# Order of the steps around the convolution, the last tiles of the dense stage and experts 0 and 1, in an adaptive-norm, gated-recurrence and mixture-of-experts block

## Chip, cores and metric

One core of one Trainium2 chip. The time is device time in microseconds (us) from start to end of one execution. Before the change it is 294.07 us, the median of three runs (293.27 to 294.33).

## What is computed

Four sequences of 256 tokens with 256 features (1024 tokens). A conditioning vector gives six modulation rows per sequence. Then

```python
h = layernorm(x) * (1 + ca) + sa
x = x + ga * attn(h)
h = layernorm(x) * (1 + cb) + sb
x = x + gb * ffn(h)
...
# attn: xn = rmsnorm(x); left = gelu(xn @ left_W + left_b)
#       right = rg_lru(causal_depthwise_conv(xn @ right_W + right_b), ...)
#       x1 = left * right @ out_W + out_b + x
#       mlp = gelu(x1n @ up1_W + up1_b) * (x1n @ up2_W + up2_b) @ down_W + down_b
#       return mlp + x1
# ffn:  8 experts, the best 2 of each token, weights renormalised:
#       hmid = gelu(tokens @ w1[e] + b1[e]); out_e = hmid @ w2[e] + b2[e]
#       combined += cw[:, e] * out_e;  return combined + hidden_states
```

## The kernel before

The program is written engine by engine; each of the five instruction streams runs in the order of the text, and semaphores (`wait_ge`, `then_inc`) tie them. Tokens come in two halves of 512 (`hf` 0 and 1), features in two tiles of 128 (`dt`). A class `Order` hands out the eight PSUM banks ahead of time: `take(key)` gives a product its bank and the counts of `filled` and `drained` to wait for; `begin(key)` waits for that bank.

*Split products.* The second dense part and the experts multiply in three parts, hi times hi, lo times hi, hi times lo. hi is ScalarE's rounding copy (`m_hi`, `v_hi_of`, `w1_hi_of`, `w2_hi_of`, `x_hi`, `own_hi_of`), lo the subtraction of it from the whole, on GpSimd for `wm_lo` and most `v_lo` (L2043), on VectorE for the experts' weights (`w1_lo_of` L1810, `w2_lo_of` L1815), their rows (`x_lo` L1916) and their hidden values (`own_lo_of` L1920, L1921).

*First part.* VectorE scales the tokens of a half (`ln_apply`, L1479), TensorE turns them (`x_blocks`), ScalarE takes squares and TensorE their mean (`mean_square`, L627), right and left products follow (L691). VectorE's convolution (`conv`, L1576) has three steps per feature tile, six per half; the gate products of that half (`gates`, L691) wait for `conv_done`. Meanwhile GpSimd splits the 8 bias rows of the experts (`b2_split`, two copies L2049 and one subtraction L2043) and then makes `wm_lo` of up1 and up2.

*End of the dense stage.* `down(1, ...)` (L788) needs the twelve v tiles of both halves; `x2_of` (L1704) adds the result to the residual. TensorE turns the sums to rows and makes router logits (`x2_and_logits`, L813, L818), VectorE chooses experts and slots. `rest(i)` (L1834, L1835) adds h times the gate row to the base rows of two token tiles; it needs `gbb`, the gate rows on all partitions, which SyncE copies there through DRAM. GpSimd scatters each token's row to its two experts in DRAM (`scatter`, L2068). Expert 0's rows are not read back: TensorE gathers them with one-hot products (`gather`, L891) from `picks` (L1825) into two banks `("x0", dt)`.

*Experts.* Each has at most 320 rows in three tiles (128, 128, 64). SyncE loads a megabyte of w1 and one of w2 per expert (`load_w1` L494, `load_w2` L497) into one staging buffer each, and the expert's rows with their slot data (`load_x`, L532 to L536). TensorE turns the rows (`turn_of`, L994), runs the first layer (`first_layer`, L1007) and the second (`second_layer`, L1050 for the whole tiles, L1043 and L1044 for the 64-row tile). ScalarE applies the gelu (`own_gelu`, L1376). VectorE multiplies the result by gate weight and gate row (`keep_y`, L1935, L1938), for which GpSimd has gathered `gb_rows` (L2099). GpSimd adds the rows into the output (L2109), once SyncE has stored the base rows there (L552). From expert 1 on, the loops of all engines run one expert's first layer ahead of the second layer of the one before. In the order of the text, TensorE does expert 0 so:

```python
first_layer(0)
pe.wait_ge(b2_ready, 1)
second_layer(0, range(ST - 1))
turn_of(1)
second_layer(0, [ST - 1])
first_layer(1, EARLY, lambda: turn_of(2))
```

If a count of more than 320 rows turns up, another branch runs all experts on all tokens; it isn't taken here.

Of the kernel before, what the change touches and what calls it, by code (L numbers as in the profile page):

```python
# [60 lines left out]
def adaln_block(nc, I, out):  # L61
# [6 lines left out]
    NH = T // HT  # L68
# [120 lines left out]
    def take_at(key, n, drains=1):  # L189
        order.take(key, drains=drains, bank=(first_bank + n) % 8)  # L190
    take_at(("x0", 0), 3, 0)
    take_at(("x0", 1), 1, 0)
    take_at(("xh2", 1, 0), 0, KD)
# [10 lines left out]
    with ctx:  # L204
# [259 lines left out]
        def _(sp):  # L464
# [31 lines left out]
            def load_w2(e):  # L496
                sp.dma_start(e_raw2[:].rearrange("p (e k n) -> p e k n", e=1, k=KE), w2v[:, bass.ds(e, 1)]).then_inc(raw2_in, 16)  # L497
# [25 lines left out]
            with sp.If(ov == 0):  # L523
# [14 lines left out]
                sp.wait_ge(w2_lo_done, 1)  # L538
                load_w2(1)
                for t in range(TT):  # L540
                    sp.wait_ge(a_scattered[t], 16)
                load_x(0)
                sp.wait_ge(w1_lo_done, 2)
                load_w1(2)
                for t in range(TT):
# [44 lines left out]
        def _(pe):  # L590
# [348 lines left out]
            down(1, [0])  # L939
            down(1, [1], lambda: x2_and_logits(1, 0))  # L940
            x2_and_logits(1, 1)
            begin(("x0", 0))
            for j in range(TH):
                gather(0, 0, j)
# [109 lines left out]
            with pe.If(ov == 0):  # L1054
# [4 lines left out]
                def turn_of(e):  # L1059
                    pe.wait_ge(xe_in[e % 2], 32 * ((e + 1) // 2))  # L1060
                    turn(e % 2)
                first_layer(0)
                pe.wait_ge(b2_ready, 1)
                second_layer(0, range(ST - 1))
                turn_of(1)
                second_layer(0, [ST - 1])
                first_layer(1, EARLY, lambda: turn_of(2))
                for e in range(1, E):
# [21 lines left out]
        def _(act):  # L1090
# [302 lines left out]
            with act.If(ov == 0):  # L1393
# [9 lines left out]
                own_blocks(0)  # L1403
                w2_hi_of(1)
                x_hi(1)
                act.wait_ge(rest_done, TT // 2)
                keep_low(0)
                w1_hi_of(2)
                own_blocks(1, lambda: x_hi(2))
                for e in range(1, E - 1):  # L1410
# [14 lines left out]
        def _(dve):  # L1425
# [454 lines left out]
            v_of(KF + 5)  # L1880
            rest(0)
            dve.wait_ge(v_lo_done, NH * KF - 1)
# [4 lines left out]
            pick(0)  # L1887
            rest(1)
            x2_of(1, [1])
# [20 lines left out]
            with dve.If(ov == 0):  # L1910
# [30 lines left out]
                for f in range(KE):  # L1941
                    own_lo_of(0, f)
                rest(2)
                keep_y(0, 0)
                rest(3)
                keep_y(0, 1)
                x_lo(1)
                keep_y(0, 2)
                w2_lo_of(1)
                for f in range(KE):  # L1950
                    if f == 2:
                        w1_lo_of(2)
                    if f == 4:
                        x_lo(2)
                    own_lo_of(1, f)
                for e in range(1, E):
                    if e + 1 < E:
# [19 lines left out]
            with dve.Else():  # L1977
                st.n = at_branch
                nc.vector.memset(cwT[0:64, :], 0.0).then_inc(cw_cleared, 1)
                rest(2)  # L1980
                rest(3)
                for i in range(TT // 2):
# [27 lines left out]
        def _(pool):  # L2010
# [31 lines left out]
            def lo(dst, whole, hi, done):  # L2042
                nc.gpsimd.tensor_tensor(dst, whole, hi.bitcast(F32), ALU.subtract).then_inc(done, 1)  # L2043

            pool.wait_ge(ffn_in, 16 * 4)
            pool.wait_ge(blank_done, 2)
# [5 lines left out]
            pool.wait_ge(b2_ready, 1)  # L2052
            for n in range(2):
                pool.wait_ge(wm_hi_done, n + 1)
                lo(wm_lo[:, n], raw_m[:, n], wm_hi[:, n], wm_lo_done)
            pool.wait_ge(conv_done, NH * KH)
            marks = h2_rows[:].bitcast(I32)
# [88 lines left out]
```

## Time and profile before

| what | value |
|---|---|
| median of three runs | 294.07 us |
| the profiled execution's own time | 293.69 us |
| its span | 291.9 us |
| TensorE matmul busy | 265.9 us, 91% of the span |
| VectorE busy | 200.3 us, 69% |
| ScalarE busy | 174.2 us, 60% |
| GpSimd busy | 128.9 us, 44% |
| mean granted clock of TensorE | 0.959 |

The span is the time between the first and the last record of the profile; the execution's own time is 1.8 us longer. The granted clock is a share of TensorE's full speed: 1.00 is its level of 2.4 GHz, 0.50 that of 1.2 GHz, and a value between is a stretch with both. The chain of waits follows the work that ended last back from the end; the timeline lists one engine's instructions, and at the end of a row, in brackets, how long the engine stood idle before it and for whom.

### The profile page before, as it was taken

Reading aid. Unit: us, or ns where it says so; the run is one execution under the profiler, and the core shown is the slowest. Engines: PE = TensorE matmul, PEld = TensorE weight load, DVE = VectorE, ACT = ScalarE, POOL = GpSimd, SP = SyncE. Lnnn points to the kernel's source line nnn. Section 1 sums busy time; section 2 is a strip of 40 time slices with the busy share of each in tenths; the row PEclk is TensorE's granted clock in tenths of the full one; section 3 lists DMA queues with packets and bytes.
Section 4 is the critical chain, followed back from the end, with each engine's and each line's share of the span. In section 5 each row is a group of like instructions: output and inputs, shape, how many; then the busy total and the mean of one; then the engine's idle time right before and its main releaser. Section 6 shows DMA issues by size and latency. Waiting matters only on the chain.

```text
span 291.9 us, 4510 instructions
## 1 busy us (share of the span) xinstructions
PE 265.9 (91%) x1594; PEld 222.6 (76%) x1594; DVE 200.3 (69%) x459; ACT 174.2 (60%) x295; POOL 128.9 (44%) x104
## 2 busy tenths in 40 slices
PE   7997499999999999988999588999999999999970
PEld 2745246457788788866689588999999999999970
DVE  3659778937957777779877069685867676786520
ACT  4348449596089346960789139766859393939100
POOL 7009300000051312368075528738483839476651
PEclk9979599999999999999799869999999999999997
DMA  6990000000003757316145964929395766627233
GB/s 193 381 299 1 2 1 0 0 0 2 0 2 103 268 161 165 69 57 212 41 140 172 289 195 97 342 53 325 103 295 141 241 196 190 189 33 203 23 38 37
DMA packets 32838, 38.40 MB, mean 132 GB/s; under 512 B 7964, under 2 KB 28444, under 8 KB 32796
## 3 DMA queue, kind: packets, MB, share of 16 engines
q1 hardware_dynamic: 27184, 30.56, 33.4%
q0 software_dynamic: 4928, 7.44, 11.3%
q8 instruction: 15, 0.25, 0.3%
q10 hardware_dynamic: 700, 0.07, 0.2%
q14 instruction: 11, 0.09, 0.1%
HBM read 32.10 MB, written 8.90 MB: 140 GB/s over the span
## 4 chain that ended last, share of the span: by engine, by line
PE 50%; DVE 19%; DMA 9%; SPq 8%; issue 5%; ACT 4%; POOL 2%; POOLq 1%; DVEq 0%; ACTq 0%
PE bank L1007 15%; PE bank L1050 12%; PE bank L691 9%; SPq L505 5%; DVE u L1576 5%; PE bank L1044 3%; DMA x_rows<-blank 2%; PE bank L1043 2%; PE bank L891 2%; DMA gb_rows<-gb_table,meta 2%; DVE w_lo L1815 2%; DVE w_lo L1810 2%; SPq L509 1%; DMA x_tok<-in_L_attn_x 1%; PE bank L635 1%
## 5 line engine op out<-in xcount | busy, mean ns | idle before, releaser
L2109 POOL DMA_INDIRECT out_x<-y_tok,meta x24 | 53.3, 2219 | 38.2 <-DVE y_tok L1938 25.9
L1050 PE MATMUL bank<-w_hi,own 128*128 128x256 f32 x256 | 48.2, 283 | 0.0
L1920 DVE TENSOR_TENSOR own<-own_raw,own 128x256 fp32r<-128x256 f32 x64 | 27.2, 425 | 21.5 <-issue 13.2
L1007 PE MATMUL bank<-xe_hi,w_hi 128*128 128x320 f32 x128 | 39.9, 312 | 1.1 <-DVE xe_lo L1916 1.1
L1050 PEld LDWEIGHTS bank<-w_hi,own 128*128 128x128 f32 x256 | 40.9, 191 | 0.0
L1376 ACT ACTIVATE own_raw<-bank,b1c 128x320 f32<-128x320 f32 x64 | 33.5, 534 | 10.8 <-PE bank L1007 10.5
L1007 PE MATMUL bank<-xe_lo,w_hi 128*128 128x320 f32 x128 | 39.6, 309 | 0.0
L1007 PE MATMUL bank<-xe_hi,w_lo 128*128 128x320 f32 x128 | 39.6, 309 | 0.0
L1050 PE MATMUL bank<-w_lo,own 128*128 128x256 f32 x128 | 36.2, 283 | 0.0
L1382 ACT ACTIVATE own<-own_raw 128x320 fp32r<-128x320 f32 x64 | 29.8, 482 | 0.0
L2099 POOL DMA_INDIRECT gb_rows<-gb_table,meta x24 | 24.5, 1020 | 11.5 <-issue 6.7
L1007 PEld LDWEIGHTS bank<-xe_hi,w_hi 128*128 128x128 f32 x128 | 24.0, 188 | 1.4 <-issue 1.3
L1050 PEld LDWEIGHTS bank<-w_lo,own 128*128 128x128 f32 x128 | 24.4, 191 | 0.0
L1007 PEld LDWEIGHTS bank<-xe_lo,w_hi 128*128 128x128 f32 x128 | 24.0, 188 | 0.1
L1007 PEld LDWEIGHTS bank<-xe_hi,w_lo 128*128 128x128 f32 x128 | 24.0, 188 | 0.0
L2043 POOL TENSOR_TENSOR v_lo<-tmp,v_hi 128x512 fp32r<-128x512 f32 x6 | 7.8, 1300 | 35.4 <-ACT v_hi L1227 35.4
L691 PE MATMUL bank<-u,raw_a 128*128 128x512 f32 x32 | 15.9, 648 | 5.4 <-DVE u L1576 5.4
L1938 DVE SCALAR_TENSOR_TENSOR y_tok<-bank,meta,gb_rows 128x256 f32<-128x256 f32 x16 | 7.7, 484 | 17.3 <-PE bank L1050 9.8
L616 PE MATMUL bank<-n_hi,wm_hi 128*128 128x512 f32 x46 | 18.9, 412 | 0.0
L1810 DVE TENSOR_TENSOR w_lo<-e_raw,w_hi 128x2048 fp32r<-128x2048 f32 x8 | 18.3, 2282 | 0.0
L1815 DVE TENSOR_TENSOR w_lo<-e_raw,w_hi 128x2048 fp32r<-128x2048 f32 x8 | 18.2, 2281 | 0.0
L1390 ACT ACTIVATE low_rows<-bank 64x256 f32<-64x256 f32 x8 | 3.0, 381 | 25.4 <-PE bank L1044 25.4
(248 smaller groups left out, 636.5 us busy)
## 6 DMA issues: line engine op xcount, KB each, us to landing
e_raw<-in_L_ffn_w SPq DMA_DIRECT2D x16, 1024.0 KB
x_rows<-in_L_attn_x SPq DMA_DIRECT2D x1, 2560.0 KB
xe_tok<-x_rows SPq DMA_DIRECT2D x7, 256.0 KB
raw_m<-in_L_attn_up_W SPq DMA_DIRECT2D x2, 768.0 KB, 9.9
x_tok<-in_L_attn_x SPq DMA_DIRECT2D x2, 512.0 KB, 5.3
out_x<-x_tok SPq DMA_DIRECT2D x1, 1024.0 KB, 5.3
xe_tok<-x_rows SPq DMA_DIRECT2D x7, 128.0 KB
wmod<-in_L_wmod SPq DMA_DIRECT2D x1, 768.0 KB, 12.2
```

What stands on the lines that cost most here:

```text
L505: sp.dma_start(out_rows[T:T + CAP], xr[0:CAP]).then_inc(spare_in, 16)
L616: ins = nc.tensor.matmul(ps[:, 0:n], l, r, start=(c == 0 and t == 0), stop=(c == k - 1 and t == 2))
L691: ins = nc.tensor.matmul(ps[:], raw_a[:, n, c, m * P:(m + 1) * P], x[:, c, hs[hf]], start=(c == 0), stop=(c == KD - 1))
L1007: ins = nc.tensor.matmul(bank[b][:, 0:CAP], l, r, start=(c == 0 and t == 0), stop=(c == KD - 1 and t == 2))
L1050: ins = nc.tensor.matmul(bank[b][0:n, 0:D], l, r, start=False, stop=(c == KE - 1 and t == 2))
L1376: nc.scalar.activation(own_raw[:, f % 4, :], bank[b][:, 0:CAP], ACT.Gelu, bias=b1c[:, g:g + 1]).then_inc(drained[b], 1)
L1382: nc.scalar.activation(own_hi[e % 2][:, f, :], own_raw[:, f % 4, :], ACT.Copy).then_inc(own_hi_done, 1)
L1810: nc.vector.tensor_tensor(w1_lo[e % 2][:], e_raw1[:].rearrange("p (k n) -> p k n", k=KD), w1_hi[e % 2][:].bitcast(F32), ALU.subtract).then ...
L1815: nc.vector.tensor_tensor(w2_lo[e % 2][:], e_raw2[:].rearrange("p (k n) -> p k n", k=KE), w2_hi[e % 2][:].bitcast(F32), ALU.subtract).then ...
L1920: nc.vector.tensor_tensor(own_lo[e % 2][:, f, :], own_raw[:, f % 4, 0:whole], own_hi[e % 2][:, f, 0:whole].bitcast(F32), ALU.subtract)
L2099: nc.gpsimd.indirect_dma_start(gb_rows[e % 2][0:n, k, :], None, gb_table, bass.IndirectOffsetOnAxis(ap=ids[0:n, e, k, E + 1:EXTRA], axis=0 ...
L2109: nc.gpsimd.indirect_dma_start(out_rows, bass.IndirectOffsetOnAxis(ap=ids[0:n, e, k, E:E + 1], axis=0), y_tok[e % 2][0:n, k, :], None, com ...
```

## The change

Nothing is computed otherwise; steps move on all five engines and two banks are exchanged.

```diff
-    take_at(("x0", 0), 3, 0)
-    take_at(("x0", 1), 1, 0)
+    take_at(("x0", 0), 1, 0)
+    take_at(("x0", 1), 3, 0)
...
                 sp.wait_ge(w2_lo_done, 1)
                 load_w2(1)
+                sp.wait_ge(w1_lo_done, 2)
+                load_w1(2)
                 for t in range(TT):
                     sp.wait_ge(a_scattered[t], 16)
                 load_x(0)
-                sp.wait_ge(w1_lo_done, 2)
-                load_w1(2)
...
             down(1, [1], lambda: x2_and_logits(1, 0))
+            begin(("x0", 0))
+            gather(0, 0, 0)
             x2_and_logits(1, 1)
-            begin(("x0", 0))
-            for j in range(TH):
+            for j in range(1, TH):
                 gather(0, 0, j)
...
                 turn_of(1)
+                first_layer(1, EARLY, lambda: turn_of(2))
                 second_layer(0, [ST - 1])
-                first_layer(1, EARLY, lambda: turn_of(2))
...
                 own_blocks(0)
                 w2_hi_of(1)
+                w1_hi_of(2)
                 x_hi(1)
+                own_blocks(1, lambda: x_hi(2))
                 act.wait_ge(rest_done, TT // 2)
                 keep_low(0)
-                w1_hi_of(2)
-                own_blocks(1, lambda: x_hi(2))
...
             v_of(KF + 5)
-            rest(0)
             dve.wait_ge(v_lo_done, NH * KF - 1)
...
             pick(0)
-            rest(1)
             x2_of(1, [1])
...
                 for f in range(KE):
                     own_lo_of(0, f)
+                rest(0)
+                rest(1)
                 rest(2)
+                x_lo(1)
                 keep_y(0, 0)
                 rest(3)
                 keep_y(0, 1)
-                x_lo(1)
-                keep_y(0, 2)
-                w2_lo_of(1)
                 for f in range(KE):
                     if f == 2:
                         w1_lo_of(2)
                     if f == 4:
                         x_lo(2)
                     own_lo_of(1, f)
+                keep_y(0, 2)
+                w2_lo_of(1)
...
+            for n in range(2):
+                pool.wait_ge(wm_hi_done, n + 1)
+                lo(wm_lo[:, n], raw_m[:, n], wm_hi[:, n], wm_lo_done)
+            pool.wait_ge(conv_done, NH * KH)
             pool.wait_ge(ffn_in, 16 * 4)
             pool.wait_ge(blank_done, 2)
...
             pool.wait_ge(b2_ready, 1)
-            for n in range(2):
-                pool.wait_ge(wm_hi_done, n + 1)
-                lo(wm_lo[:, n], raw_m[:, n], wm_hi[:, n], wm_lo_done)
-            pool.wait_ge(conv_done, NH * KH)
```

`conv_done` is waited for with the count of both halves, so the bias rows come behind all twelve convolution steps. The branch for more than 320 rows does rest(0) and rest(1) too now; it isn't taken.

How the instructions stand on three engines, before and after. On GpSimd, in the first part of the program, before:

```order
L2036 IOTA blank 128x3
L2049 TENSOR_SCALAR b_split<-b_row 8x256 x2
L2043 TENSOR_TENSOR b_split<-b_row,b_split 8x256
L2043 TENSOR_TENSOR wm_lo<-raw_m,wm_hi 128x1536 x2
L2058 IOTA h_rows 128x8
```

and now (the lines of the changed file are one to five further down):

```order
L2037 IOTA blank 128x3
L2044 TENSOR_TENSOR wm_lo<-raw_m,wm_hi 128x1536 x2
L2054 TENSOR_SCALAR b_split<-b_row 8x256 x2
L2044 TENSOR_TENSOR b_split<-b_row,b_split 8x256
L2059 IOTA h_rows 128x8
```

The three bias operations went behind the two weight subtractions. On TensorE, at the end of `down(1, [1])`, one piece of the difference (L891 is a gather; L813 and L818 are x2_and_logits):

```order
 L788 MATMUL bank<-v_hi,wm_lo 128x512
+L891 MATMUL bank<-picks,h_rows 128x320
 L813 MATMUL bank<-ident,xT 128x128 x4
 L818 MATMUL bank<-rt,xT 128x8 x4
-L891 MATMUL bank<-picks,h_rows 128x320 x5
+L891 MATMUL bank<-picks,h_rows 128x320 x4
 L829 MATMUL bank<-ident,xhat_118 128x128 x4
```

One of the five gathers went ahead of the turning of the last sums. On VectorE, behind expert 0's eight hidden-value subtractions (`bits` and `x_tok` are a rest, `y_tok` is keep_y, `xe_lo_144` is x_lo(1), `w_lo_133` is w2_lo_of(1)), before:

```order
L1834 TENSOR_TENSOR bits<-h_rows,gbb 128x512
L1835 TENSOR_TENSOR x_tok<-x_tok,bits 128x512
L1938 SCALAR_TENSOR_TENSOR y_tok_148<-bank,meta,gb_rows_137 128x256
L1834 TENSOR_TENSOR bits<-h_rows,gbb 128x512
L1835 TENSOR_TENSOR x_tok<-x_tok,bits 128x512
L1938 SCALAR_TENSOR_TENSOR y_tok_148<-bank,meta,gb_rows_137 128x256
L1916 TENSOR_TENSOR xe_lo_144<-bank,xe_hi_142 128x320 x2
L1935 TENSOR_TENSOR y_tok_148<-bank,low_rows 64x256
L1938 SCALAR_TENSOR_TENSOR y_tok_148<-y_tok_148,meta,gb_rows_137 64x256
L1815 TENSOR_TENSOR w_lo_133<-e_raw_111,w_hi_132 128x2048
```

and now, behind the first two of three rests:

```order
L1835 TENSOR_TENSOR bits<-h_rows,gbb 128x512
L1836 TENSOR_TENSOR x_tok<-x_tok,bits 128x512
L1915 TENSOR_TENSOR xe_lo_144<-bank,xe_hi_142 128x320 x2
L1937 SCALAR_TENSOR_TENSOR y_tok_148<-bank,meta,gb_rows_137 128x256
L1835 TENSOR_TENSOR bits<-h_rows,gbb 128x512
L1836 TENSOR_TENSOR x_tok<-x_tok,bits 128x512
L1937 SCALAR_TENSOR_TENSOR y_tok_148<-bank,meta,gb_rows_137 128x256
L1919 TENSOR_TENSOR own_136<-own_raw,own_136 128x256
```

x_lo(1) went ahead of both keep_y, and the last keep_y and w2_lo_of(1) behind expert 1's own subtractions.

## Rows read from the trace of the kernel before

**Rows 1.** Chain of waits, in order of time: start us, us, what.

```profile
163.54 4.78 DMA gb_rows<-gb_table,meta
...
192.67 2.88 PE bank L1050 x24
197.54 7.04 PE bank L1007 x48
```

**Rows 2.** Timeline of VectorE: start us, us, engine line op out<-in xcount [idle before].

```profile
18.03 1.38 DVE L1479 TENSOR_SCALAR xhat<-x_tok,mv,rstd 128x256 f32<-128x256 f32 x4
21.55 11.29 DVE L1576 SCALAR_TENSOR_TENSOR u<-rbuf,cols,u 128x512 f32<-128x512 f32 x6 [2.13 <-ACT u L1164]
...
21.55 0.75 DVE L1576 SCALAR_TENSOR_TENSOR u<-rbuf,cols,u 128x512 f32<-128x512 f32 x1 [2.13 <-ACT u L1164]
...
45.62 4.57 DVE L1576 SCALAR_TENSOR_TENSOR u<-rbuf,cols,u 128x512 f32<-128x512 f32 x6
...
95.52 1.31 DVE L1691 TENSOR_SCALAR tmp<-hT,cols,mod 128x256 f32<-128x256 f32 x1
...
159.69 0.69 DVE L1834 TENSOR_TENSOR bits<-h_rows,gbb 128x512 f32<-128x512 f32 x1
...
174.28 2.28 DVE L1815 TENSOR_TENSOR w_lo<-e_raw,w_hi 128x2048 fp32r<-128x2048 f32 x1
```

**Rows 3.** Timeline of GpSimd.

```profile
21.23 1.80 POOL L2049 TENSOR_SCALAR b_split<-b_row 8x256 fp32r<-8x256 f32 x2 [13.29 <-DMA b_row<-in_L_ffn_b]
23.11 0.72 POOL L2043 TENSOR_TENSOR b_split<-b_row,b_split 8x256 fp32r<-8x256 f32 x1
23.91 7.60 POOL L2043 TENSOR_TENSOR wm_lo<-raw_m,wm_hi 128x1536 fp32r<-128x1536 f32 x2
...
95.38 2.59 POOL L2043 TENSOR_TENSOR v_lo<-tmp,v_hi 128x512 fp32r<-128x512 f32 x2 [2.04 <-ACT v_hi L1227]
```

**Rows 4.** Timeline of ScalarE.

```profile
16.21 1.48 ACT L1110 ACTIVATE wm_hi<-raw_m 128x1536 fp32r<-128x1536 f32 x1 [0.90 <-issue]
...
22.97 1.94 ACT L1141 ACTIVATE square<-bank,mod 128x256 f32<-128x256 f32 x4
...
139.33 1.93 ACT L1273 ACTIVATE xhat<-bank,centred,rstd 128x256 f32<-128x256 f32 x4 [0.63 <-issue]
```

**Rows 5.** Timeline of TensorE, matmuls.

```profile
25.83 1.84 PE L627 MATMUL bank<-small,square 128*128 128x1 f32 x16
32.89 3.43 PE L691 MATMUL bank<-u,raw_a 128*128 128x512 f32 x4 [5.22 <-DVE u L1576]
...
37.05 5.32 PE L691 MATMUL bank<-u,raw_a 128*128 128x512 f32 x12
...
128.78 0.47 PE L788 MATMUL bank<-v_hi,wm_hi 128*128 128x512 f32 x1 [1.06 <-DVE v_lo L1884]
...
136.05 0.83 PE L813 MATMUL bank<-ident,xT 128*128 128x128 f32 x4 [0.92 <-DVE xT L1704]
...
137.53 4.63 PE L891 MATMUL bank<-picks,h_rows 128*128 128x320 f32 x10
...
166.43 1.54 PE L994 MATMUL bank<-ident,xe_tok 128*128 128x128 f32 x6 [2.94 <-DMA xe_tok<-x_rows]
...
181.63 0.39 PE L1007 MATMUL bank<-xe_hi,w_hi 128*128 128x320 f32 x1 [1.09 <-DVE xe_lo L1916]
```

**Rows 6.** Busy time by stretches (PEclk is TensorE's granted clock).

```profile
32.80:34.50 1.70, 1.61 (x2) 0.84 (x3) 1.70 (x5) 0.00 (x0) 0.00 (x0) 0.50 0.04 10
...
139.00:141.00 2.00, 2.00 (x5) 1.29 (x4) 1.82 (x7) 1.67 (x4) 0.00 (x0) 0.50 0.27 98
```

**Rows 7.** Timeline of SyncE's queue.

```profile
158.29 0.65 SPq L494 DMA_DIRECT2D e_raw<-in_L_ffn_w  x1
160.78 0.37 SPq L532 DMA_DIRECT2D xe_tok<-x_rows  x1
```

**Rows 8.** DMA issues: KB each, median us from issue to landing.

```profile
gbb<-gb_table SPq DMA_DIRECT2D x1, 512.0 KB, 3.5
```

More of the change, by code:

```diff
@@ L1979, in _ @@
                 nc.vector.memset(cwT[0:64, :], 0.0).then_inc(cw_cleared, 1)
-                rest(2)
-                rest(3)
+                for i in range(TT // 2):
+                    rest(i)
                 for i in range(TT // 2):
```

## Prediction

> **What bounds the kernel now.** I read the chain of waits in order of time first, then the timeline of each engine where that chain leaves TensorE, then the granted clock there. Times are microseconds (us) of the old trace. From 182 on the chain is TensorE alone: each later expert takes it some 15.7 us, first layers 7.04 and a tile of the second layer 2.88 [rows 1], with no wait worth removing. So the change can gain only before that, at three places.
>
> *Convolution (17 to 36).* VectorE's six convolution steps take 11.29 us; the six of the other half take 4.57 [rows 2]. The 6.7 us between lie beside GpSimd's two wm_lo subtractions, 7.60 together [rows 3]. TensorE has finished the mean square at 27.67 and waits 5.22 us; the next product then runs four matmuls in 3.43 [rows 5], at granted clock 0.50, the 1.2 GHz level [rows 6].
>
> *Last part of the dense stage (125 to 150).* VectorE does rest(0) before the last v_lo, and rest(1) before x2_of(1,[1]). TensorE waits 1.06 for the one, then 0.92 for the other, and the five gathers behind (ten records) run 4.63 [rows 5], mostly at clock 0.50 [rows 6].
>
> *Expert 0 to expert 1 (163 to 182).* TensorE stands 2.94 us until expert 1's rows land at 166.4 [rows 5]. SyncE asked for them at 160.78, behind expert 2's 1 MB of w1 at 158.29 [rows 7]. Then VectorE waits for the gathered gb rows until 168.3 [rows 1], and x_lo(1) and the third tile stand behind that. First layer 2 starts at 181.63 [rows 5].
>
> **Part 1, bias rows behind the convolution.** wm_lo(0) no longer stands behind the bias rows (21.23 to 23.83 [rows 3]). It starts when ScalarE's wm_hi(0) ends, 16.21 + 1.48 = 17.69 [rows 4], and holds 3.80 us, to about 21.56. At 18.03 VectorE wants the four token scalings of half 1, L1479, 1.38 us [rows 2]. Are they held? A tensor_scalar from SBUF of the same shape took 1.31 at 95.52 instead of about 0.35, beside v_lo [rows 2, 3]. So yes: they end near 22.75 instead of 19.4. TensorE's transposes wait 1.3 us for them (22.85 instead of 21.52); left products and mean square shift too, and the latter ends at 27.67 + 1.3 = 28.95. The convolution runs 22.75 + 4.57 = 27.3, unheld, so TensorE goes on at 28.95 instead of 32.89: 3.95 saved. It has no 5 us hole before it; I take the clock to stay up: four matmuls then need 1.8 (a third of the 5.32 that twelve take at full clock behind it [rows 5]) instead of 3.43: 1.6 saved.
> What comes back: wm_lo(1) needs wm_hi(1), which trails the squares. From the end of the scalings, L: transposes and handover 0.6, squares 1.8 (1.94 less their overlap with the copy), copy 1.48 [rows 4], handover 0.07: request at L + 3.95. The sixth convolution step starts at L + 3.8, five sixths of the 4.57 behind. It is ahead by some 0.2, which is thin (first rival). The bias rows now run near 45, beside the scan. The first convolution step took 0.75 beside the bias copies at 21.23 [rows 2, 3], so these hold nothing; the 0.72 subtraction may hold up to 0.72, I take 0.35. TensorE's out products wait for that VectorE work. Sum of part 1: 3.95 + 1.6 - 0.35 = **5.2**; bounds 1.4 (the race lost, no clock) and 5.7.
> In the Trainium skill, "SBUF — State Buffer", section "Who interferes with whom", a VectorE operation with two SBUF inputs contends with any GpSimd one that reads SBUF, so the bias copies would hold the scan as well, and part 1 would be worth up to 1.8 less. The 0.75 row speaks against it.
>
> **Part 2, rests inside expert 0; gather 0 early.** Without rest(0) the last v_lo is there when TensorE comes: its wait of 1.06 goes. rest(1) (two operations of 0.69 [rows 2]) ended some 0.5 behind down(1,1); the rest of the 0.92 is x2_of's own first half. So the transposes behind start 1.6 sooner, at 134.45 instead of 136.05 [rows 5], and VectorE's statistics, logits and choice with them. gather(0,0,0), in the bank that up2 left free, fills what is left of the hole. The other four gathers are eight records; they start at 137.53 - 1.6 = 135.9, and if the clock stays at 2.4 GHz take about half of 8 x 0.46, 1.9: till 137.8, not 142.16. xhat2_rows(0) then waits for the second of ScalarE's four norm rows, 139.33 + half of 1.93 [rows 4], less 1.6: 138.7. TensorE's part leads by 3.3 there, VectorE's and ScalarE's own by 1.6; slots, picks and modulate_last wait for both in turn, and I put the picks of half 1, on which the last gathers hang, at 2.5. Sum: **2.5**; bounds 1.6 (VectorE's lead alone) and 3.3 (TensorE's).
>
> **Part 3, expert 1 first.** w1 of expert 2 is asked for when w1_lo(1) is done, 153.7, not at 158.29 [rows 7], so it travels under first layer 0. It passes load_x(0) and the second-half scatters, and shares the engines with them; I charge 0.3 for a later last scatter. Without a megabyte ahead, the 384 KB of expert 1 asked for at 160.78 need some 3.5 us (the 512 KB of gbb took 3.5 [rows 8]): landed at 164.3 instead of 166.4, 2.1 saved. VectorE: eight own_lo, then rests 0 to 2 from 159.69, six operations of 0.69 [rows 2], to 164.0: x_lo(1) is not late. TensorE then: turn 0.7, handover to xe_lo 1.0, first layer 1 7.04, turn(2) 0.7, third tile 2.9 = 12.3, to 176.6. The old stretch 166.43 to 181.63 was 15.2: 2.9 saved. Behind the gb wait, now: y 0.48, rest(3) 1.4, y 0.48, two own_lo 1.2, w1_lo(2) 2.28 [rows 2], two more 1.0, x_lo(2) 0.9 = 7.8 us; with gb rows at 168.3 as before it ends at 176.1, just hidden. keep_y(0,2) and w2_lo(1) end near 181, second layer 1 wants them at 184.3: hidden by 3 us. The base rows leave at 169.5 instead of 170.4. Sum: 2.1 + 2.9 - 0.3 = **4.7**; bounds 2 and 5.5.
>
> Total 5.2 + 2.5 + 4.7 = 12.4. Against the profiled execution (293.69; 1.8 outside its span of 291.9) 281.3; it stood 0.38 under the median 294.07, which gives 281.7. I say **281.5**.
>
> **Rivals.**
> (a) *The race is lost*: wm_lo(1) is ahead of the last convolution step, holds it 3.8 us, TensorE starts at 31.2, perhaps cold; part 1 is 1.4: 285.3. For: the margin is 0.2 in 4. Against: both chains hang on the same L, so the margin doesn't depend on when they start. Chance 0.22.
> (b) *Expert 1's rows come no sooner*: w1(2) slows the scatters by the 2 us it saves, or two holes of 1 us before first layer 1 bring the clock down to 1.2 GHz as at 139 [rows 6]. Part 3 is 2: 284.2. Chance 0.20.
> (c) *The bias copies hold the scan*, as the rule above would have it: 1.8 more, 283.3. Chance 0.08.
> (d) *Slower*: VectorE's queue. The wait for gb rows now stands ahead of all own_lo(1), w1_lo(2) and x_lo(2). Those rows may land up to 168.8 for nothing; each us later costs one. At 181.2 the gain is gone, at 183 the kernel takes 295.9. For: it did wait for them before. Against: before, they were there at 168.3 with a megabyte in front. Chance 0.02.
> (e) *Nothing comes through*: VectorE or GpSimd (the out additions) paces the experts and swallows the lead: 294. Against: TensorE runs through from 182 on [rows 1]. Chance 0.02.
>
> **How the numbers follow.** Forecast 0.46, (a) 0.22, (b) 0.20, (c) 0.08, (d) 0.02, (e) 0.02. Range: (a) with (b) is 288; both bounds up are 279. I take 278.5 to 287. A measurement tells 0.5% (1.5 us) here; all but (d) and (e) lie beyond: faster 0.96, same 0.02, slower 0.02.
>
> **What would show it.** Right: L1479 near 4.7 instead of 1.38, six convolution steps near 4.6, no wait before the gate products; no wait at the last v_lo, gathers at clock 1.0; turn of expert 1 near 157 (164.3 + 0.3 - 7.7), first layer 2 near 169 (176.9 - 7.7). Wrong: a convolution step of 3 us or more (a); w1(2) still travelling when expert 1's rows are asked for (b); a wait of VectorE for gb rows over 10 us (d).

## The result, and the profile after

The changed kernel takes **284.82 us** (median of 4 runs, 283.95 to 286.46), the kernel before, beside it, 294.20 (293.27 to 294.83): ratio 0.969, 95% interval 0.963 to 0.975. Faster, as forecast, and inside the range; but the gain is 9.4 us where I had said 12.5. The profiled execution took 283.95 us, its span is 282.2 (291.9 before). Of a kernel's runs, those more than 1.5% above its fastest are left out of every median, range and ratio of this document. Names and line numbers below are those of the changed kernel, up to five away from the old ones.

Convolution and the recurrence behind it, timeline of VectorE, then of GpSimd, kernel after (start us, us, engine line op out<-in):

```profile
18.00 4.23 DVE L1480 TENSOR_SCALAR xhat<-x_tok,mv,rstd 128x256 f32<-128x256 f32 x4
22.16 4.56 DVE L1577 SCALAR_TENSOR_TENSOR u<-rbuf,cols,u 128x512 f32<-128x512 f32 x6
...
45.33 0.84 DVE L1630 TENSOR_TENSOR ui<-ui,tmp 128x512 f32<-128x512 f32 x1
46.21 1.81 DVE L1633 TENSOR_TENSOR_SCAN ui<-tmp,ui 128x256 f32<-128x256 f32 x2
```

```profile
17.69 3.43 POOL L2044 TENSOR_TENSOR wm_lo<-raw_m,wm_hi 128x1536 fp32r<-128x1536 f32 x1 [9.89 <-ACT wm_hi L1111]
26.43 3.57 POOL L2044 TENSOR_TENSOR wm_lo<-raw_m,wm_hi 128x1536 fp32r<-128x1536 f32 x1 [5.31 <-ACT wm_hi L1111]
44.29 1.79 POOL L2054 TENSOR_SCALAR b_split<-b_row 8x256 fp32r<-8x256 f32 x2 [14.29 <-DVE u L1577]
46.16 0.72 POOL L2044 TENSOR_TENSOR b_split<-b_row,b_split 8x256 fp32r<-8x256 f32 x1
```

Beside [rows 2, 3]: the six convolution steps take 4.56 instead of 11.29 us, the four token scalings 4.23 instead of 1.38, as the prediction had it (4.7). The sixth step starts near 25.96, wm_lo(1) at 26.43: the race is won by 0.47. The two then overlap, and the step, which began first, is not held.

TensorE, timeline, kernel after, against [rows 5] (its own lines; those of the experts are the turn and first matmul of expert 1):

```profile
26.66 1.84 PE L627 MATMUL bank<-small,square 128*128 128x1 f32 x16
28.36 1.96 PE L691 MATMUL bank<-u,raw_a 128*128 128x512 f32 x4
...
158.24 1.28 PE L995 MATMUL bank<-ident,xe_tok 128*128 128x128 f32 x6 [2.71 <-DMA xe_tok<-x_rows]
160.21 0.61 PE L1008 MATMUL bank<-xe_hi,w_hi 128*128 128x320 f32 x1 [0.69 <-ACT xe_hi L1368]
```

The gate products start at 28.36, not 32.89, and at full clock. Later they lead by 6.0, and after the bias rows by 5.3 (from 63 to 124 us of the old trace): the product of 0.84 took 0.69 before, the scan of 1.81 took 1.27.

SyncE's queue after, against [rows 7]; then the chain of waits after:

```profile
145.83 0.37 SPq L494 DMA_DIRECT2D e_raw<-in_L_ffn_w  x1
...
155.09 0.37 SPq L532 DMA_DIRECT2D xe_tok<-x_rows  x1
```

```profile
149.73 5.28 DMA x_rows<-h_rows,slot_b
155.51 2.61 DMA xe_tok<-x_rows
158.24 1.29 PE bank L995 x6
160.21 6.98 PE bank L1008 x30
167.84 2.64 PE bank L1008 x18
172.46 7.04 PE bank L1008 x48
...
188.12 7.04 PE bank L1008 x48
```

Busy time by stretches after (stretch, length, busy us and count of PE, PEld, DVE, ACT, POOL, granted clock, DMA share, GB/s):

```profile
158.00:160.00 2.00, 1.28 (x6) 0.88 (x6) 0.49 (x1) 0.87 (x2) 0.69 (x1) 0.64 0.82 177
160.00:162.00 2.00, 1.79 (x7) 1.82 (x8) 0.49 (x1) 0.00 (x0) 1.54 (x2) 0.50 0.53 147
162.00:164.00 2.00, 2.00 (x9) 2.00 (x9) 1.93 (x4) 0.00 (x0) 1.57 (x2) 0.50 0.38 113
164.00:166.00 2.00, 2.00 (x12) 2.00 (x11) 0.33 (x1) 1.14 (x3) 0.00 (x0) 0.65 0.66 220
```

Where the time went: at 142.13 us, when expert 0's first layer starts (150.07 before), the lead is 7.94, which is parts 1 and 2 almost as forecast (7.7). It is 9.4 at the row of 188.12 (197.54 before [rows 1]), and stays there. So part 3 brought 1.5 us instead of 4.7. Two things stand in these rows: the last scatter, issued at 149.73, needs 5.28 us to land, so that SyncE asks for expert 1's rows at 155.09; and TensorE, after 2.71 us without work, runs the turn of expert 1 and the start of its first layer mostly at the 1.2 GHz level until 166 (granted clock 0.50 to 0.65), thirty matmuls in 6.98 us.

### The profile page after: what moved, and what is told of

Read it like the earlier page. It is cut to its first block, busy times and chain, and to the rows that moved or that the text cites. A ratio compares the mean times of both kernels' runs of the same rounds, so it can differ in the third digit from the quotient of the medians.

```text
span 282.2 us, 4509 instructions
## 1 busy us (share of the span) xinstructions
PE 263.2 (93%) x1593; PEld 221.2 (78%) x1594; DVE 196.1 (69%) x459; ACT 174.2 (62%) x295; POOL 127.9 (45%) x104
## 4 chain that ended last, share of the span: by engine, by line
PE 65%; DVE 13%; DMA 5%; POOL 5%; issue 4%; ACT 4%; POOLq 1%; SPq 0%; DVEq 0%; ACTq 0%
PE bank L1008 18%; PE bank L1051 12%; PE bank L691 9%; PE bank L616 6%; PE bank L788 5%; POOL x_rows L2069 3%; PE bank L1045 2%; PE bank L1044 2%; DMA x_rows<-h_rows,slot_b 2%; PE bank L995 2%; DVE u L1577 2%; PE bank L627 2%; DVE xhat L1480 1%; PE bank L635 1%; DMA x_tok<-in_L_attn_x 1%
## 5 line engine op out<-in xcount | busy, mean ns | idle before, releaser
L2110 POOL DMA_INDIRECT out_x<-y_tok,meta x24 | 52.7, 2196 | 35.8 <-DVE y_tok L1937 24.1
L1919 DVE TENSOR_TENSOR own<-own_raw,own 128x256 fp32r<-128x256 f32 x64 | 27.2, 426 | 21.4 <-issue 11.9
L1008 PE MATMUL bank<-xe_hi,w_hi 128*128 128x320 f32 x128 | 41.1, 321 | 0.7 <-ACT xe_hi L1368 0.7
L1008 PE MATMUL bank<-xe_lo,w_hi 128*128 128x320 f32 x128 | 40.5, 317 | 0.0
L1008 PE MATMUL bank<-xe_hi,w_lo 128*128 128x320 f32 x128 | 40.5, 317 | 0.0
L2100 POOL DMA_INDIRECT gb_rows<-gb_table,meta x24 | 24.4, 1017 | 12.5 <-issue 6.4
L1008 PEld LDWEIGHTS bank<-xe_hi,w_hi 128*128 128x128 f32 x128 | 25.0, 195 | 1.1 <-issue 1.1
L1008 PEld LDWEIGHTS bank<-xe_lo,w_hi 128*128 128x128 f32 x128 | 25.0, 196 | 0.1
L1008 PEld LDWEIGHTS bank<-xe_hi,w_lo 128*128 128x128 f32 x128 | 24.9, 195 | 0.0
L2044 POOL TENSOR_TENSOR v_lo<-v_more,v_hi 128x512 fp32r<-128x512 f32 x5 | 6.4, 1289 | 26.2 <-ACT v_hi L1228 26.2
L616 PE MATMUL bank<-n_hi,wm_lo 128*128 128x512 f32 x46 | 18.0, 391 | 0.0
L616 PE MATMUL bank<-n_lo,wm_hi 128*128 128x512 f32 x46 | 17.9, 390 | 0.0
```

Of the source, the lines that this page charges most:

```text
L616: ins = nc.tensor.matmul(ps[:, 0:n], l, r, start=(c == 0 and t == 0), stop=(c == k - 1 and t == 2))
L1008: ins = nc.tensor.matmul(bank[b][:, 0:CAP], l, r, start=(c == 0 and t == 0), stop=(c == KD - 1 and t == 2))
L1919: nc.vector.tensor_tensor(own_lo[e % 2][:, f, :], own_raw[:, f % 4, 0:whole], own_hi[e % 2][:, f, 0:whole].bitcast(F32), ALU.subtract)
L2100: nc.gpsimd.indirect_dma_start(gb_rows[e % 2][0:n, k, :], None, gb_table, bass.IndirectOffsetOnAxis(ap=ids[0:n, e, k, E + 1:EXTRA], axis=0 ...
L2110: nc.gpsimd.indirect_dma_start(out_rows, bass.IndirectOffsetOnAxis(ap=ids[0:n, e, k, E:E + 1], axis=0), y_tok[e % 2][0:n, k, :], None, com ...
```

## The experiments

**How they are read.** Single runs of one kernel lie 2 to 5 us apart, in part because the opening takes longer in some: the first convolution step starts at 22.16 us in one profile and at 24.47 or 24.63 in others. So beside the medians I use two lengths inside each profile: **A**, from the first convolution step to the first matmul of expert 0's first layer, and **B**, from there to that of expert 3's first layer, behind which all profiles are alike (94.2 to 94.8 us to the end). "Low clock" is where B's granted clock is under 0.7. A, B and the low clock are of one profiled execution each, and that isn't always a typical one. It is the slowest of six of busy_hole (286.19) and of combined (283.58), and the second slowest of x_first (286.26); it is the fastest of part3_undone (283.71), x_first_late (281.82), rests_back (283.14) and bias_later (281.72).

| kernel | runs kept | median us (runs from, to) | ratio to before, 95% | A | B | low clock in B |
|---|---|---|---|---|---|---|
| before | 4 of 4 | 294.20 (293.27, 294.83) | | 128.52 | 47.31 | 166 to 172 |
| after | 4 of 4 | 284.82 (283.95, 286.46) | 0.969 (0.963, 0.975) | 119.97 | 45.83 | 158 to 166 |
| part1_only | 6 of 6 | 290.01 (288.73, 290.25) | 0.986 (0.980, 0.991) | 121.46 | 47.98 | 164 to 170 |
| sub_beside_conv | 6 of 6 | 289.26 (287.68, 290.38) | 0.983 (0.977, 0.989) | 121.51 | 45.17 | 168 to 170 |
| x_first | 4 of 6 | 284.39 (281.05, 285.06) | 0.965 (0.957, 0.974) | 121.00 | 46.68 | 166 to 170 |
| busy_hole | 5 of 6 | 282.12 (281.02, 284.05) | 0.961 (0.955, 0.967) | 119.87 | 45.33 | 164 to 166 |
| after_again | 6 of 6 | 285.49 (283.82, 285.87) | 0.969 (0.965, 0.974) | 119.99 | 45.74 | 160 to 166 |
| part3_undone | 6 of 6 | 285.96 (283.71, 287.70) | 0.973 (0.968, 0.978) | 119.94 | 44.44 | none |
| busy_both | 6 of 6 | 282.81 (281.84, 283.98) | 0.962 (0.957, 0.967) | 119.97 | 43.76 | none |
| x_first_late | 6 of 6 | 284.48 (281.82, 285.79) | 0.967 (0.962, 0.972) | 119.96 | 43.86 | none |
| rests_back | 4 of 6 | 286.24 (283.14, 286.72) | 0.975 (0.970, 0.980) | 121.48 | 43.13 | none |
| bias_later | 7 of 7 | 285.00 (281.72, 285.82) | 0.967 (0.964, 0.971) | 119.28 | 44.20 | 158 to 162 |
| x_first_third | 3 of 6 | 281.39 (280.80, 283.16) | 0.957 (0.950, 0.963) | 119.73 | 42.64 | none |
| combined | 6 of 6 | 282.21 (280.81, 283.58) | 0.956 (0.953, 0.960) | 119.07 | 45.33 | 164 to 168 |

The three groups of four (part1_only to busy_hole, after_again to x_first_late, the last four) each ran beside the kernel before on one chip. The other three runs of x_first_third took 285.65, 285.76 and 669 us, the last far outside everything else. With all six its median is 284.40, so its row is the least sure of the table.

**Part 1 alone (part1_only).** The kernel before, with GpSimd's order changed and nothing else:

```
+            for n in range(2):
+                pool.wait_ge(wm_hi_done, n + 1)
+                lo(wm_lo[:, n], raw_m[:, n], wm_hi[:, n], wm_lo_done)
+            pool.wait_ge(conv_done, NH * KH)
             pool.wait_ge(ffn_in, 16 * 4)
...
             pool.wait_ge(b2_ready, 1)
-            for n in range(2):
-                pool.wait_ge(wm_hi_done, n + 1)
-                lo(wm_lo[:, n], raw_m[:, n], wm_hi[:, n], wm_lo_done)
-            pool.wait_ge(conv_done, NH * KH)
```

> The kernel before with nothing but part 1: the bias rows' two copies and one subtraction on GpSimd stand behind the wait for the sixth convolution step instead of ahead of wm_lo(0). The theory (part 1 is worth the 5.15 us by which the changed kernel leads at its second half) gives 294.2 - 5.2 = 289.0 us, with TensorE at 2.4 GHz through the gate products and no convolution step over 0.8 us. The rival, that the lead is partly given back because the rows of expert 1 wait for the scatters and the chain's transfers in any case, gives 291 or more.

290.01 beside 293.80 for the kernel before on the same chip. By the ratio 0.986 part 1 is worth 4.2 us, with an interval of 2.6 to 5.9. The theory's 5.2 is inside it and so is the rival's 3.2, so the times alone don't decide between them; the length A, below, is clearer. A reader who looks only at the end misses one thing. Granted clock around the gathers of expert 0 (stretches as above), first before, then with part 1 alone:

```profile
138.00:140.00 2.00, 2.00 (x6) 1.33 (x5) 1.72 (x11) 0.97 (x3) 0.85 (x1) 0.56 0.67 251
140.00:142.00 2.00, 2.00 (x6) 1.16 (x5) 1.57 (x7) 1.98 (x4) 0.00 (x0) 0.59 0.04 15
```

```profile
134.00:136.00 2.00, 2.00 (x14) 1.68 (x13) 1.83 (x10) 0.30 (x1) 1.66 (x2) 1.00 0.96 372
136.00:138.00 2.00, 2.00 (x11) 1.48 (x11) 1.79 (x8) 1.54 (x4) 0.00 (x0) 1.00 0.27 98
```

The full clock that I had put down to part 2 was there with part 1 alone, although TensorE's waits of 1.1 and 0.9 us ahead of it still stood (rests_back, below, with 1.1 and 0.4, shows the same). So A shrinks by 7.06 us. Up to the last v_lo, at 124 us of the old trace, it has shrunk by 5.95. In the kernel after, 0.61 of the same amount is not gained, since the first step itself starts later there (22.16 against 21.55), which leaves 5.3 (the 5.15 of the expectation is 5.3 by these rows). The other 1.1 comes at the gathers, with this clock. Why the clock is up there with part 1 and was down before, no run shows. B is 0.7 longer, with a low stretch as before.

**A second subtraction, meant to run beside the first convolution steps (sub_beside_conv).** wm_lo(0) is subtracted twice:

```
+            pool.wait_ge(wm_hi_done, 1)
+            nc.gpsimd.tensor_tensor(wm_lo[:, 0], raw_m[:, 0], wm_hi[:, 0].bitcast(F32), ALU.subtract).then_inc(pool_step, 1)
+            pool.wait_ge(pool_step, 2)
             for n in range(2):
```

> The changed kernel with wm_lo(0) subtracted twice on GpSimd (the first result is overwritten by the same numbers), so that a subtraction of 3.4 us runs from 21.1 us on, beside VectorE's convolution steps from 22.2. This is the race of part 1 lost on purpose. Theory (a subtraction of GpSimd holds the convolution step that starts under it to its own end): the step at 22.2 ends about 24.7 instead of 22.9, what follows is 1.8 to 2.4 us later, wm_lo(1) then starts at 26.4 and holds a further step for up to 3 us more, and the time is 287 to 290 us. Rival (the hold of before came from its own cause, the copies' place or the clock): every step stays at 0.76 us and the time is 284.8.

Timeline of VectorE with the double subtraction, and of GpSimd:

```profile
20.09 7.22 DVE L1480 TENSOR_SCALAR xhat<-x_tok,mv,rstd 128x256 f32<-128x256 f32 x4
...
27.24 4.55 DVE L1577 SCALAR_TENSOR_TENSOR u<-rbuf,cols,u 128x512 f32<-128x512 f32 x6
```

```profile
19.59 3.42 POOL L2047 TENSOR_TENSOR wm_lo<-raw_m,wm_hi 128x1536 fp32r<-128x1536 f32 x1 [11.74 <-ACT wm_hi L1111]
23.10 3.42 POOL L2044 TENSOR_TENSOR wm_lo<-raw_m,wm_hi 128x1536 fp32r<-128x1536 f32 x1
31.97 3.44 POOL L2044 TENSOR_TENSOR wm_lo<-raw_m,wm_hi 128x1536 fp32r<-128x1536 f32 x1 [5.45 <-ACT wm_hi L1111]
```

The time came out as expected (3.8 us over after_again, in another group), the place did not. In this profile the subtraction met the token scalings, not the convolution: four take 7.22 us beside two subtractions, where they took 4.23 beside one. The convolution starts 2.8 us later than in busy_hole, whose opening was as late (24.47), and the gate products 4.4 later (34.98 against 30.61). In these rows VectorE waits out each of GpSimd's subtractions. That a *convolution step* is held is shown by the profile before alone. In no profile with part 1 in it did wm_lo(1) start before the sixth step did. In six of them (after, after_again, busy_both, x_first_late, rests_back, bias_later) it started 0.47 behind it and overlapped its end: the step kept its 0.75 us, and wm_lo(1) took 3.57 to 3.60 instead of 3.43.

**Expert 1's rows ahead of expert 2's weights (x_first).** SyncE's order and, with it, ScalarE's:

```
                 load_w2(1)
-                sp.wait_ge(w1_lo_done, 2)
-                load_w1(2)
...
                 load_x(1)
+                sp.wait_ge(w1_lo_done, 2)
+                load_w1(2)
...
-                w1_hi_of(2)
                 x_hi(1)
+                w1_hi_of(2)
```

> The changed kernel with expert 1's rows asked for before expert 2's first weights (which are then rounded by ScalarE after the rows of expert 1, still ahead of its first gelu). Theory: w1(2), asked for at 145.83, shared the DMA engines with the last scatters, which took 5.28 us instead of 3.37. Then the scatters land in about 3.4 us here, the rows come some 1.9 us sooner, TensorE's idle time ahead of the turn of expert 1 falls from 2.7 to about 0.8 us, its clock stays at 2.4 GHz in the first layer of expert 1 (2.6 us more), and the time is 281 to 283 us. Rival: the scatters are as slow without w1(2) beside them, since their own issue on GpSimd and their small packets set them; then the rows come no sooner, and w1(2), 512 KB or more behind them, comes late for VectorE's third convert: 285 to 287 us.

Neither, by the runs kept: 284.39 us. The rows came sooner and TensorE's wait for them fell to 0.2 us, but a new wait took its place. Timeline of TensorE, then of ScalarE, in x_first:

```profile
156.78 0.87 PE L995 MATMUL bank<-ident,xe_tok 128*128 128x128 f32 x6 [0.19 <-issue]
...
166.37 0.64 PE L1008 MATMUL bank<-xe_hi,w_hi 128*128 128x320 f32 x1 [3.58 <-ACT own_raw L1377]
```

```profile
163.99 1.91 ACT L1290 ACTIVATE w_hi<-e_raw 128x2048 fp32r<-128x2048 f32 x1 [5.48 <-DMA e_raw<-in_L_ffn_w]
165.81 0.93 ACT L1377 ACTIVATE own_raw<-bank,b1c 128x320 f32<-128x320 f32 x2
```

The weights, asked for at 155.33 beside the rows of experts 1 and 2, landed at 164, and ScalarE stood in front of them with the gelus of expert 1 behind. This profile is of a run of 286.26 us, at a mean clock of 0.972. The four runs kept, 281.05 to 285.06 at 0.979 to 0.986, have no profile, so how long this wait is in them isn't shown.

**The same, with the weights used later (x_first_late, x_first_third).** ScalarE rounds them behind its fourth gelu of expert 1; VectorE subtracts them ahead of row 5, in x_first_third ahead of row 3.

> Expert 1's rows ahead of expert 2's first weights, as in x_first, but with ScalarE rounding those weights behind the fourth gelu of expert 1 and VectorE's subtraction behind its sixth row, so that weights that land 8.7 us after they are asked for (155.3 to 164.0) hold up nothing. Theory: TensorE's 3.6 us wait for own_raw of x_first is gone, no idle time ahead of the turn is left, and the clock stays up but for a dip; first layer 2 starts 2 to 3 us sooner than in the unedited kernel, measured from the start of expert 0's first layer: 282 us. Rival: the weights' rounding in the middle of the gelus, 1.9 us, and their subtraction ahead of the next expert's first layer stall TensorE for as long again: 284 to 286 us.

> As x_first_late, with VectorE's subtraction of expert 2's first weights two rows sooner (ahead of the fourth row of expert 1, right after ScalarE has rounded them). There TensorE stood 2.6 us ahead of expert 2's first layer until that subtraction ended at 169.85 us. Theory: it ends near 166.6 and the wait falls from 2.6 to 1 us or less; from the first layer of expert 0 to that of expert 3 it takes 42.2 us in place of 43.86 (45.74 in the unedited kernel), and the time is 283 us, with the clock up in most runs. Rival: the wait moves to the rows of expert 1 that now come 2.3 us later (ScalarE's eighth gelu waits for the fourth subtraction), and the time is that of x_first_late, 284.5.

The 3.6 us wait is gone. In x_first_late TensorE waits 2.6 us at expert 2's first layer for VectorE's subtraction, in x_first_third 1.1, and B falls from 45.8 to 43.86 and 42.64, the shortest of all (I expected 42.2). The times follow less clearly: x_first_late, 284.48, is level with the change; x_first_third, 281.39, is under it (0.957 beside 0.969), but by three runs of six. Mean clocks of the six runs of x_first_late are 0.982 to 0.985 in three and 0.970 to 0.972 in three, so its low stretch comes and goes.

What these runs settle is the scatters. When the weights are asked for, against the issue of the last scatter, and the time from that issue to SyncE's next request, which waits for its landing:

| kernel | weights asked for | from last scatter's issue to the rows' request |
|---|---|---|
| x_first_late | behind the rows | 149.17 to 151.97: 2.80 us |
| part1_only | 0.89 after it | 153.42 to 156.70: 3.28 |
| before | 0.88 after it | 157.41 to 160.78: 3.37 |
| after | 3.90 ahead of it | 149.73 to 155.09: 5.36 |
| part3_undone | 0.24 ahead of it | 150.28 to 156.20: 5.92 |

The other profiles agree: 2.6 to 2.8 us in the four with the weights behind the rows, 5.0 to 6.0 in the seven with the change's order. A megabyte that is under way, or starts just ahead, costs the last scatter 1.6 to 2.7 us over one that starts 0.9 us behind it, and 2.2 to 3.3 over none.

**Part 3 taken back (part3_undone).** SyncE, ScalarE, VectorE and the third tile as before, the first two rests where the change put them.

> The changed kernel with part 3 taken back (expert 2's first weights asked for after the meta rows of expert 0 again, the third tile of expert 0 ahead of expert 1's first layer, ScalarE's and VectorE's orders there as before, but the first two rests still behind expert 0's products); parts 1 and 2 stay. The prediction put part 3 at 4.7 us, which would give 289.5 us. The theory from the trace (rows 1.9 us later by slower scatters, and the clock at 1.2 GHz in expert 1's first layer) puts it at 1.4 to 2 us: 286.2 to 286.8 us. A rival that it is worth nothing gives 284.8 us.

285.96 beside 285.49, ranges on top of each other: **part 3 brings nothing that these runs can tell**, 0.5 us by the medians and 1.1 by the ratios where 4.7 was forecast. In the profile, its fastest run, B is even 1.3 shorter than after_again's: the clock stayed up through a wait of 3.3 and one of 1.0 us. Its mean clock was 0.980 there and 0.967 to 0.976 in the other five runs, so they are not shown to have kept it. It is no exact return to the old order: there the weights were asked for behind the last scatter, here 0.24 ahead of it, and the rows are asked for at 156.20, later than after's 155.09.

**The clock (busy_hole, busy_both).** Unread matmuls where TensorE waits:

```
+                for _ in range(12):
+                    nc.tensor.matmul(bank[4][:], all_ones[:], all_ones[:, 0:1].to_broadcast([P, HT]), start=True, stop=True)
                 turn_of(1)
+                b, _, need = order.at[("s1", 0)]
+                pe.wait_ge(drained[b], KE // 4 + need)
+                for _ in range(6):
+                    nc.tensor.matmul(bank[b][:], all_ones[:], all_ones[:, 0:1].to_broadcast([P, HT]), start=True, stop=True)
                 first_layer(1, EARLY, lambda: turn_of(2))
```

This is busy_both; busy_hole has eleven ahead of the turn and none behind.

> The changed kernel with eleven matmuls of 512 columns that nothing reads, into a free bank, between the second tile of expert 0 and the wait for expert 1's rows (TensorE waits there for 2.71 us; eleven at 0.22 us are 2.4). It takes no wait away and moves no transfer. Theory: what part 3 failed to bring is mostly the clock, 1.2 GHz from 158 to 166 us, set by this idle time; kept busy, TensorE runs the turn and the first layer of expert 1 at 2.4 GHz, 2.6 + 0.6 us less, and 3 us of it reach the end: 281.8 us. Rival: the first layer of expert 1 would end no sooner, since VectorE's wait for gb_rows and ScalarE's gelus pace what follows: 284 to 285 us.

> The changed kernel with twelve unread matmuls of 512 columns ahead of the turn of expert 1 and six more behind it, while TensorE waits for the first half of expert 1's rounded rows. With eleven ahead alone TensorE still stood 0.7 us for the rows and 1.0 us for xe_lo, and its clock fell to 1.2 GHz from 163 to 166 us. Theory (the clock follows these idle times): now it stays at 2.4 GHz through the first layer of expert 1, which then takes some 4.4 us of its first 30 matmuls in place of 7, and the time is 1.5 to 3 us under that of the unedited kernel, 282 to 283.3. Rival (what paces there is ScalarE and VectorE, or the clock falls whatever TensorE runs): 284 to 285 us.

busy_both against after_again, on one chip: 282.81 against 285.49 (of the other's six runs only the fastest, 283.82, is under the slowest of these, 283.98), mean clock 0.982 to 0.985 in all six against 0.967 to 0.975. It does more work, asks for nothing sooner (the rows at 155.29, not 154.77), and is 2.7 us faster; B is 2.0 shorter. Timeline of TensorE, stretches and two rows of the chain of waits, busy_both:

```profile
158.63 0.88 PE L995 MATMUL bank<-ident,xe_tok 128*128 128x128 f32 x6 [0.37 <-issue]
159.34 1.47 PE L1072 MATMUL bank<-all_ones 128*128 128x512 bf16 x6
160.50 0.46 PE L1008 MATMUL bank<-xe_hi,w_hi 128*128 128x320 f32 x1
```

```profile
158.00:160.00 2.00, 1.63 (x12) 1.00 (x10) 0.24 (x1) 0.77 (x2) 0.79 (x1) 1.00 0.69 143
160.00:162.00 2.00, 2.00 (x14) 1.72 (x13) 0.82 (x3) 0.00 (x0) 1.12 (x2) 1.00 0.61 180
162.00:164.00 2.00, 2.00 (x15) 2.00 (x15) 1.93 (x4) 0.96 (x3) 1.70 (x2) 1.00 0.40 113
```

```profile
160.81 4.39 PE bank L1008 x30
...
170.50 7.04 PE bank L1008 x48
```

Fourteen and fifteen matmuls in a stretch where after had seven and nine, and thirty in 4.39 us instead of 6.98. With the first hole alone filled (busy_hole), the profile shows waits of 0.7 and 1.0 us left and a low clock from 163 to 166: only 0.5 us of B. But that is its run of 286.19 us. Its other five have mean clocks of 0.977 to 0.985 and a median of 282.12, at a ratio of 0.961 beside busy_both's 0.962. By the times the first hole alone is worth as much as both, and nothing shows that the second had to be filled.

**Part 2 taken back (rests_back).** rest(0) ahead of the last v_lo, rest(1) behind pick(0); the gathers as changed.

> The changed kernel with the first two base rows, rest(0) and rest(1), back in their old places on VectorE, ahead of the last v_lo and behind pick(0); the order of the gathers and all else as changed. The theory of the prediction (part 2 is worth 2.5 us, which the trace of the changed kernel puts at 2.6 to 2.9) gives 285.5 + 2.7 = 288.2 us, with expert 0's first layer 2.7 us later against the first convolution step. Rival: the rests are hidden there too, or what they cost is made up behind them, since TensorE waits for expert 1's rows in any case: under 286.5 us.

TensorE's wait at the last v_lo is back. TensorE, waits in rests_back (what waited, for what: us in total, times, longest):

```profile
PE bank L995 <- DMA xe_tok<-x_rows: 2.4, 1, 2.4
PE bank L788 <- DVE v_lo L1885: 1.1, 1, 1.1
PE bank L1008 <- DVE xe_lo L1917: 1.0, 1, 1.0
...
PE bank L813 <- DVE xT L1705: 0.4, 1, 0.4
```

A is 1.5 longer, not 2.7; by the median the time is 0.7 longer and by the ratio 1.6 (286.24 and 0.975, against 285.49 and 0.969 in another group). Between the two theories, nearer to the rival. A is that of part1_only (121.48 and 121.46), so the gather moved ahead brought nothing there without the rests.

**The bias rows 12 us later (bias_later).** One wait, `until_drained(("out", 0, KD - 1))`, ahead of them on GpSimd; they ran at 56.17 (expected: 8 us later).

> The changed kernel with the two copies and the subtraction of the bias rows a further 8 us later on GpSimd, behind VectorE's last read of the first half's products, where VectorE waits 2.9 us for ScalarE's root. Theory (the subtraction of 0.72 us holds VectorE's scan at 46 us by 0.54 and the product by 0.15): the scan is back at 1.27 us for two, the recurrence 0.69 us shorter, and the whole 0.5 to 0.7 us: 284.8 to 285.0 beside 285.5. Rival (those operations are as long without GpSimd beside them, or the wait behind them takes it back): 285.5 us.

Timeline of VectorE, bias_later:

```profile
45.26 0.69 DVE L1630 TENSOR_TENSOR ui<-ui,tmp 128x512 f32<-128x512 f32 x1
45.98 1.27 DVE L1633 TENSOR_TENSOR_SCAN ui<-tmp,ui 128x256 f32<-128x256 f32 x2
```

0.84 is back to 0.69 and 1.81 to 1.27, and A is 0.69 shorter: 0.15 + 0.54, exactly. The median is 0.5 lower (285.00), not to be told from nothing by itself.

**All together (combined).** x_first_third, bias_later, `pool.wait_ge(conv_done, KH * n)` ahead of wm_lo(n), five unread matmuls behind the turn of expert 1.

> x_first_third and bias_later together, with wm_lo(1) made to wait for the first half's sixth convolution step (the race of part 1 then can't be lost) and five unread matmuls behind the turn of expert 1, in its 1.0 us wait for xe_lo. Theory: the savings add, 285.5 less 2.5 to 3.5 (sooner rows, no wait for weights, clock at 2.4 GHz in every run) less 0.6: 281.5 to 282.5 us, under both kernels and with less spread. Rival: the gains overlap in the waits for gb_rows and the weights, and it ties with x_first_third at 283 or more.

**282.21 us, 280.81 to 283.58: ratio 0.956 (0.953 to 0.960)**, under both kernels and 2.6 us under the change. busy_both (282.81) is level with it, and so is x_first_third by its ratio (0.957): that the pieces add up is not shown, and the rival stands, though at a lower time than it gave. Its profile, of its slowest run, shows what is left: TensorE waits 3.0 us for expert 2's rows, which SyncE now asks for behind the weights. Whether they belong ahead of them was not tried.

## Why the prediction was right and wrong

**Part 1 (5.2): right**, 5.3 in the trace by 118, and alone on the chip 4.2 with 5.2 inside the interval (2.6 to 5.9). All its links stand in the rows: scalings held (4.23; I said 4.7), convolution free, no hole, full clock. Its wrong figures are small and cancel, which is luck. wm_lo takes 3.43 to 3.57, not 3.80; TensorE went on at 28.36, where I had 28.95; and the bias rows cost 0.69, where I charged 0.35. Rival (a), the lost race, did not happen in any profile; the margin was 0.46 or more where I had 0.2.

**Rival (c), refuted.** Beside the two bias copies of 1.79 us VectorE lost 0.15 (0.84 against 0.69), beside the subtraction of 0.72 it lost 0.54; bias_later gives both back. The scan itself never met the copies, which ended at 46.08, 0.13 ahead of it; what did were that product, the operation ahead of it (0.69, as ever) and the first convolution step before [rows 2], 0.75. The rule of the Trainium skill, "SBUF — State Buffer", section "Who interferes with whom", holds in these rows for GpSimd's subtraction and not for its copies of eight partitions; the measurement decides.

**Part 2 (2.5): right in the sum, wrong in its make-up.** The lead grew by 2.6 between 119 and 142 in the traces. Taking the rests back costs A 1.5, where I had 1.6. The other 1.1 is the clock at the gathers, and part 1 alone already brought that, so part 2 by itself lies just below its lower bound. The step that failed is "if the clock stays at 2.4 GHz", which I credited to the removed holes: part1_only kept holes of 1.1 and 0.9 us, and the clock stayed up.

**Part 3 (4.7): the step that failed**; it was 1.5 in the traces and nothing measurable on the chip, below its bound of 2. The signs given for it missed: the turn of expert 1 came at 158.24, not near 157, and first layer 2 at 172.46, not near 169. Of its terms:

- "I charge 0.3 for a later last scatter": it was 2.0 (5.36 us from issue to request instead of 3.37). The rows themselves then came as fast as forecast: the turn starts 3.15 us after they are asked for (155.09 to 158.24), before it was 5.65. Together: the last scatter is issued 7.7 us sooner than before, the turn starts 8.2 sooner (158.24 against 166.43 [rows 5]), so 0.5 us came of 2.1 less 0.3.
- "The old stretch was 15.2, TensorE then 12.3: 2.9 saved": it took 14.2 (158.24 to 172.46). The low clock took more than the 1.9 us missing: first layer 1, costed at 7.04, took 9.6 (6.98 and 2.64 [chain of waits after]), while the third tile took 2.0 where I charged 2.9. I had the low clock only in a rival. busy_both fills the two waits and keeps the clock up: the same stretch takes 11.9 (158.63 to 170.50), under the 12.3 forecast, and B is 2.0 shorter.
- VectorE's queue behind the gb wait was no cost: it waited 1.48 us there, for gb rows that were there at 162.01, not at 168.3.

Rival (b) named both halves of this at a chance of 0.20 and gave 284.2. They are not independent of the gain: weights that travel ahead of the last scatter make it longer, and so the hole, and in the profiles of after and after_again the low clock followed that hole.

**(d) and (e)** did not happen; the lead of 9.4 us passes unchanged through six experts.

**What stays open.** What decides whether the clock falls. rests_back and after_again have the same two waits (2.4 and 1.0 us) and clock 1.00 and 0.50; part3_undone waited 3.3 and kept it. Filling the waits was enough in the profile, and the mean clock was high in all six runs; that a wait of such a length must be followed by a low clock is refuted by these two kernels. Why the clock at the gathers was down in the profile before and up with part 1 is open too. The Trainium skill, "TensorE: Matmul & The Clock Gate", section "What's actually happening", says of a kernel's start that the number of matmuls at the lower clock differs between runs of the same kernel. No run here shows that for the start; of the whole kernel, the mean clocks do differ from run to run (0.970 to 0.985, below).

## What to carry to other kernels

Moving a large load ahead of small transfers on the critical path moves its price into them: here 2 us, all that it was to save. Give the small ones the road, then place the large one's *consumer* in each engine's order by when it really lands: that gave the shortest B of all (x_first_third, 42.64), though only three of its six runs show it in the time. Where TensorE must wait, cost what follows at the lower clock too; a few unread matmuls in the hole were worth more (2.7 us) than part 3, the reordering meant to close it (0.5). And where two parts of a change lean on the same clock, cost them together, since either may bring it.

## What the chip showed beyond that

- VectorE's tensor_scalar is held by a GpSimd subtraction almost as much as its two-input operations are: four of 128x256 took 4.23 us beside one of 3.43, and 7.22 beside two, instead of 1.38. Beside two copies of 8x256 on GpSimd, a product took 0.84 instead of 0.69, and two other operations their usual time.
- A load of 1 MB asked for together with two experts' rows took 8.7 us to be usable in x_first (155.33 to 163.99) and 9.0 in combined (154.15 to 163.14), but at most 7.3 in x_first_third, where it was asked for in the same place.
- GpSimd's issue of a scatter took 0.96 us alone and 2.03 to 2.53 where it began beside VectorE's subtraction of 128x2048 (at 124.60, 139.57 and 144.61 us of the kernel after).
- The mean granted clock of one kernel differs from run to run (0.970 to 0.985 in x_first_late) with nothing changed.
